# Two head projections of a gated attention layer as the row halves of one product

## The chip, the cores and the metric

The kernel runs on one core of a Trainium2 chip. The metric is the device time of one execution in microseconds (us); where several executions are given, their median counts. A core has five engines that run their own instruction streams and meet on semaphores: TensorE (PE, matrix products into PSUM; its weight loads are listed as PEld), VectorE (DVE), ScalarE (ACT), GpSimd (POOL) and SyncE (SP), which here only starts transfers.

## What is computed

A network of two layers on an input of 4 sequences of 1024 tokens of 256 values. The change lies in the second layer's attention (`L1_attn`), of which this is the part that matters:

```python
x = _ln(x, ln1_w, ln1_b)                  # 4 x 1024 x 256
qk = _silu(x @ Wqk.T + bqk)               # 64 values a token
v = _silu(x @ Wv.T + bv)                  # 512 values a token
heads = qk[..., None, :] * gamma + beta   # four heads of 64
quad_q, lin_q, quad_k, lin_k = map(_rope, ...)
quad_att = einsum('bgid,bgjd->bgij', qq, qkk) / G + bias   # groups of 64 tokens
attn = relu(quad_att) ** 2
lin_kv = einsum('bgnd,bgne->bde', lk, vg) / n
gate = _silu(x @ Wg.T + bg)
out = (gate * (quad_out + lin_out)) @ Wo.T + bo            # then layer norm
```

`_rope(h)` is `h * cos + swapped(h) * sin` with the two halves of the 64 values exchanged in `swapped` (and a sign in `sin`). So every head needs the activated projection straight and swapped. Beside the attention the second layer has eight experts, of which each token takes two, with low-rank additions; the first layer has a causal attention and a wide feed-forward part. The sum of all is the output.

## The kernel before

All matrix products of the parts named here are fp32 split in a high and a low part (fp32r), so that one product of a 128-row block is three matmuls; with an input of 256 values (two chunks `c`) a product of 512 columns is six matmuls at L1554 (helper `times`).

The work runs in stages that follow one another on each engine: the first layer (`layer0`), the second layer's attention for sequences 2 and 3 (`attention(..., half=0)`, about 450 to 590 us of the span), the experts over 71 tiles of 128 gathered rows (`moe`, about 590 to 940 us), and the attention for sequences 0 and 1 (`half=1`, about 940 us to the end). The order inside a stage is written by hand: for each engine a table lists units such as `VV:3` or `QK:1` (`ATTENTION_UNITS`, and `TURN` where the first layer's end and the first attention half are interleaved). Within a half the two sequences make four blocks `n` of 512 tokens. The units that matter:

- `UT`: transposition of the normed rows, PE then ACT (high part) and DVE (low part, L1783) into `uT`.
- `VV:n` (16 a half): the value product of 128 tokens, DVE adds the bias (L1809), ACT applies Silu (L1721).
- `GA:n` (16 a half): the gate product of a block, ACT applies Silu into `gT` (L1729).
- `QK:n` and `QR:n` (4 each a half): the head projection, straight (`QK`, columns 0 to 127 of `wqk1`) and swapped (`QR`, columns 128 to 255). Each is 128 rows, since the 64 values stand there twice, for two heads. ACT applies Silu into `q` or `r` (L1718) and so gives the PSUM bank back.
- `QC:n`, `RS:n` (DVE, L1788): `q` times the cosine table, `r` times the sine table, in place.
- `HA:n`, `HB:n` (DVE, L1801 and L1803): `headA` and `headB` as `q*gamma + offset`, then `+ r*gamma_swapped`. `headA` holds the two query heads on partitions 0 to 63 and 64 to 127, `headB` the two key heads.
- `KT:n` (PE, L1583): `headB` is transposed; `AT:n` (L1616): the attention inside groups; `LK:n` (L1624): the sum over keys and values of a whole sequence, which waits for all eight `VV` and both `KT` of it; `OO:n` (L1634, L1637) the output rows, `YY:n` (L1648) the output projection.
- `YS`, `YF` (DVE, L1837 to L1858): the layer norm behind `YY`. Each odd `YS` has a step on POOL too, a power at L1496.
- `XB` (DVE, L1814): a bias onto the rows that the result is added to.
- `BP`, `WH`, `WL`, `FB` (first half only): the norm's weight and bias are folded into the weights.
- `GX`, `GZ` (POOL, L1486, second half only): 64 gathering transfers, each adding the expert results of 128 rows onto the rows in SBUF. POOL issues them in the order of its table, with the `YS` steps in between.

The products rotate over six PSUM banks in the order of PE's table (`g_use`): a product waits until the one six places ahead of it has been taken from its bank by ACT or DVE.

## Time and profile before

| | |
|---|---|
| median of 3 runs | 1089.68 us (1088.37 to 1092.4) |
| time of the profiled execution | 1089.73 us |
| its span | 1088.1 us |
| TensorE busy | 1050.9 us (97%) |
| VectorE busy | 797.1 us (73%) |
| ScalarE busy | 387.2 us (36%) |
| GpSimd busy | 432.8 us (40%) |
| granted TensorE clock, mean | 0.991 |

The span is measured inside the profiled execution; its time holds another 1.6 us around it. The busy share of an engine is the union of its instructions. Matmuls overlap in the pipeline, so the duration of one (some 390 ns at L1554) is longer than the step from one to the next. A line of a timeline gives the start, the time covered, the engine, source line, operation, the tile written and the tiles read, the count, and in brackets how long the engine had been idle before and what it had waited for.

### The profile page before, as it was taken

The numbers are of one execution on the slowest core, as the hardware profiler recorded it, in microseconds if no ns is written. First come the engines' busy times: TensorE is split into PE (matmuls) and PEld (weight loads), VectorE is DVE, ScalarE is ACT, GpSimd is POOL, SyncE is SP. The second block draws the span as 40 slices with busy tenths as digits, with TensorE's granted clock in tenths as the row PEclk, the third lists the DMA queues.
The fourth block names the chain that finished last, engine by engine and source line by source line (L and its number), as shares of the span: only waits on it lengthen the run. The fifth ranks groups of instructions, "written<-read, shape, count | busy, mean of one in ns | idle before, by whom it ended". The sixth has DMA issues, their size and how long they took to land.

```text
span 1088.1 us, 20660 instructions
## 1 busy us (share of the span) xinstructions
PE 1050.9 (97%) x6206; PEld 903.1 (83%) x6206; DVE 797.1 (73%) x1842; ACT 387.2 (36%) x786; POOL 432.8 (40%) x408
## 2 busy tenths in 40 slices
PE   5999999999999999999999999999999999999995
PEld 4898889887989798967877888888888888878874
DVE  5667987788788877787857877777777777754745
ACT  2644454445353535443311232323222232432300
POOL 2834666565756575163202110101001000188876
PEclk9999999999999999999999999999999999999998
DMA  8333444543445337321144565515345241355556
GB/s 253 102 117 127 139 148 141 181 161 127 157 166 175 113 134 234 120 72 41 52 142 141 199 214 170 199 50 199 103 146 192 93 161 52 113 99 89 86 79 145
DMA packets 87254, 147.83 MB, mean 136 GB/s; under 512 B 8432, under 2 KB 64624, under 8 KB 87024
## 3 DMA queue, kind: packets, MB, share of 16 engines
q1 hardware_dynamic: 66416, 98.24, 27.9%
q0 software_dynamic: 20736, 48.28, 16.1%
q8 instruction: 57, 0.93, 0.4%
q14 instruction: 45, 0.37, 0.1%
HBM read 89.04 MB, written 57.45 MB: 135 GB/s over the span
## 4 chain that ended last, share of the span: by engine, by line
PE 70%; DVE 13%; issue 7%; POOL 6%; DMA 2%; ACT 0%; DVEq 0%; POOLq 0%; ACTq 0%
PE wide L2073 18%; PE wide L592 12%; PE bank L592 11%; PE bank L2073 9%; PE bank L2098 3%; POOL first_half L1486 3%; PE wide L1554 3%; DVE hT L1022 2%; PE wide L1648 2%; PE bank L1554 2%; POOL x_second L1486 2%; PE bank L2066 1%; PE wide L1624 1%; DMA x1b<-slot_results_scratch,result_rows 1%; POOL x1b L1486 1%
## 5 line engine op out<-in xcount | busy, mean ns | idle before, releaser
L2073 PE MATMUL wide<-expert_ring,xsT 128*128 x852 | 228.5, 403 | 1.5 <-DVE xsT L2162 0.8
L2073 PEld LDWEIGHTS wide<-expert_ring,xsT 128*128 128x128 f32 x852 | 150.1, 188 | 29.3 <-issue 3.0
L2131 ACT ACTIVATE gsT<-bank 128x512 fp32r<-128x512 f32 x71 | 42.5, 599 | 243.6 <-PE bank L2098 243.6
L1946 POOL DMA_DIRECT2D expert_ring<-experts_scratch x24 | 17.1, 712 | 253.2 <-DVE slots_h L2180 186.1
L2073 PEld LDWEIGHTS bank<-expert_ring,gsT 128*128 128x128 f32 x852 | 112.1, 189 | 6.6 <-issue 0.3
L2073 PE MATMUL bank<-expert_ring,gsT 128*128 x852 | 114.0, 282 | 0.1
L2174 DVE TENSOR_TENSOR slots_h<-wide,expert_bias 128x512 f32<-128x512 f32 x71 | 49.1, 691 | 73.3 <-PE wide L2073 73.1
L563 POOL TENSOR_TENSOR folded_matrix<-fold,folded_matrix 128x512 fp32r<-128x512 f32 x48 | 64.1, 1341 | 60.6 <-ACT folded_matrix L778 60.4
L576 POOL DMA_INDIRECT slot_rows_scratch<-u,slot x64 | 66.8, 1044 | 50.1 <-issue 20.6
L592 PE MATMUL bank<-w,hT 128*128 128x264 f32 x480 | 61.5, 285 | 0.5 <-DVE hT L1022 0.5
L592 PEld LDWEIGHTS bank<-w,hT 128*128 128x128 f32 x480 | 59.5, 188 | 0.8 <-issue 0.7
L592 PE MATMUL wide<-xnT,pT 128*128 128x512 f32 (+2 forms) x288 | 59.1, 352 | 0.0
L1486 POOL DMA_INDIRECT x1b<-slot_results_scratch,result_rows x16 | 27.3, 1707 | 74.2 <-DVE x1b L1814 68.9
L2162 DVE TENSOR_TENSOR gsT<-bank,gsT 128x512 fp32r<-128x512 f32 x71 | 49.0, 690 | 9.5 <-ACT gsT L2131 1.5
L2183 DVE SCALAR_TENSOR_TENSOR slots_g<-slots_h,xs_ring,slots_h 128x512 f32<-128x512 f32 x71 | 53.4, 752 | 2.5
L1486 POOL DMA_INDIRECT first_half<-slot_results_scratch,result_rows x32 | 51.3, 1604 | 9.7 <-issue 9.3
L1022 DVE TENSOR_TENSOR hT<-hid,hT 128x512 fp32r<-128x512 f32 x64 | 53.4, 840 | 2.1 <-ACT hid L834 1.9
L2180 DVE TENSOR_TENSOR slots_h<-wide,expert_bias 128x512 f32<-128x512 f32 x71 | 49.1, 691 | 7.0 <-PE wide L2073 1.7
L592 PEld LDWEIGHTS wide<-xnT,pT 128*128 128x128 f32 x288 | 48.2, 190 | 6.3 <-issue 0.2
L592 PE MATMUL bank<-xnT,w 128*128 128x512 f32 x192 | 51.1, 409 | 0.0
L592 PE MATMUL wide<-xnT,w 128*128 128x512 f32 x192 | 50.8, 406 | 0.0
L1496 POOL TENSOR_TENSOR rsy<-vey,half 128x2 f32<-128x2 f32 x16 | 16.8, 1049 | 78.1 <-DVE vey L1846 78.1
(313 smaller groups left out, 2398.8 us busy)
## 6 DMA issues: line engine op xcount, KB each, us to landing
experts_scratch<-folded_matrix SPq DMA_DIRECT2D x24, 1024.0 KB, 5.2
expert_ring<-experts_scratch POOLq DMA_DIRECT2D x24, 1024.0 KB, 5.6
raw<-in_expert_weights SPq DMA_DIRECT2D x24, 512.0 KB, 6.2
xs_ring<-slot_rows_scratch SPq DMA_DIRECT2D x71, 128.5 KB, 2.4
slot_results_scratch<-ys_ring SPq DMA_DIRECT2D x71, 128.0 KB, 2.4
lora<-in_expert_lora SPq DMA_DIRECT2D x24, 288.0 KB, 3.1
u<-in_L_attn_x SPq DMA_DIRECT2D x4, 1024.0 KB, 5.3
expert_bias<-in_expert_bias POOLq DMA_DIRECT2D x8, 512.0 KB, 7.0
```

Of the source, the lines that this page charges most:

```text
L563: tt(fold_part(n, 1), fold[:, n % 2, :], fold_part(n, 0), ALU.subtract).then_inc(matrix_ready, 1)
L576: nc.gpsimd.indirect_dma_start(out=scr["xs"], in_=xb[:, b % 2, t, 0:ROW], in_offset=None, bounds_check=SLOTS - 1, out_offset=bass.Indirect ...
L592: ins = mm(o, stationary(i), moving(j), start=(first and q == 0), stop=(last and q == 2))
L1022: tt(hT[:, 1, n % IC, :], hid[:, n % 2, :], hT[:, 0, n % IC, :], ALU.subtract).then_inc(hid_low, 1)
L1486: nc.gpsimd.indirect_dma_start(out=target, out_offset=None, in_=scr["ys"], in_offset=index(k, tile_at), bounds_check=SLOTS_T * P - 1, comp ...
L1554: ins = mm(o, stationary(i), moving(j), start=(first and k == 0), stop=(last and k == 2))
L2073: ins = mm(o, parts[i], moving, start=(first and q == 0), stop=(last and q == 2))
L2131: return nc.scalar.activation(o, i, ACT.Copy)
L2162: tt(flat[1], bank, flat[0], ALU.subtract).then_inc(taken, 1)
L2174: tt(h1[:, j % 2, :], H[j % 2][0], bias(e, 0, HID), ALU.add).then_inc(h1_ready, 1)
L2180: tt(h3[:, i, :], H[i][1], bias(e, HID, HID), ALU.add).then_inc(h_taken, 1)
L2183: stt(out=g[:, i, :], in0=h1[:, i, :], scalar=xs[:, j % ROUND, DIM:ROW], in1=h3[:, i, :], op0=ALU.mult, op1=ALU.mult).then_inc(g_ready, 1)
```

## The change

`WEIGHTS1` gives `wqk1` 128 columns instead of 256: the 64 straight columns and then the 64 swapped ones (`heads_first`). The units `QR` are gone from all tables. One product `QK:n` of six matmuls gives the straight projection on partitions 0 to 63 and the swapped one on 64 to 127. ACT takes that bank three times: whole into `q`, the upper half into the lower half of `r`, the lower half into the upper half of `r`; the bank is given back behind the third. So `q` holds straight and swapped values, `r` swapped and straight ones, and the tables (`turn`), the scale and offset columns (`head_columns`) and the biases are laid out to fit: cosine and sine are mixed over the partitions in the same way. `headA` and `headB` hold what they held. In the tables `QK:n` stands mostly where `QR:n` or `QK:n` stood first; the DVE table is unchanged, and so are POOL's and SP's.

```diff
-WEIGHTS1 = (("wqk1", 4 * QK), ("wv1", H1), ("wg1", H1))
+WEIGHTS1 = (("wqk1", 2 * QK), ("wv1", H1), ("wg1", H1))
...
-            elif kind in ("QK", "QR"):
+            elif kind == "QK":
                 rows_split(n)
                 weight_split(0)
                 o, done = g_bank(un)
-                at = slice(0, P) if kind == "QK" else slice(P, 2 * P)
                 for c in range(DC):
-                    last = times(o, lambda i: wqk1[:, i, c, at], lambda i: uT[:, i, c, n % 2 * 512:(n % 2 + 1) * 512],
+                    last = times(o, lambda i: wqk1[:, i, c, :], lambda i: uT[:, i, c, n % 2 * 512:(n % 2 + 1) * 512],
                                  c == 0, c == DC - 1)
...
-                    for k in range(2):
-                        for c in range(DC):
-                            last = mm(S[:, 512 + EC + k:513 + EC + k], raw["wqk1"][:, c, k * P:(k + 1) * P],
-                                      cols[:, 2 + c:3 + c], start=(c == 0), stop=(c == DC - 1))
+                    for c in range(DC):
+                        last = mm(S[:, 512 + EC:513 + EC], raw["wqk1"][:, c, :], cols[:, 2 + c:3 + c],
+                                  start=(c == 0), stop=(c == DC - 1))
...
-            elif kind in ("QK", "QR"):
-                to, bias = (q, cols[:, 8:9]) if kind == "QK" else (r, cols[:, 9:10])
+            elif kind == "QK":
                 if n >= 2:
                     act.wait_ge(headB_ready, H0 + n - 1)
-                nc.scalar.activation(to[:, n % 2, :], g_full(act, un), ACT.Silu, bias=bias).then_inc(g_free(un)[0], 1)
+                both, lower, upper = g_full(act, un), slice(0, QK), slice(QK, P)
+                nc.scalar.activation(q[:, n % 2, :], both, ACT.Silu, bias=cols[:, 8:9])
+                nc.scalar.activation(r[lower, n % 2, :], both[upper], ACT.Silu, bias=cols[upper, 8:9])
+                nc.scalar.activation(r[upper, n % 2, :], both[lower], ACT.Silu, bias=cols[lower, 8:9]).then_inc(g_free(un)[0], 1)
...
             elif kind in ("QC", "RS"):
                 to = q if kind == "QC" else r
-                dve.wait_ge(*g_free(("QK" if kind == "QC" else "QR", n)))
+                dve.wait_ge(*g_free(("QK", n)))
```

PE's rows at the start of the first attention half, before (`wv`, `wg` and `wqk` with a number are the split weights; the first row is `QR:0`, the last `QR:1`; behind it come `VV:6`, `VV:7` and `KT:0`):

```order
L1554 MATMUL wide<-uT,wqk_92 128x512 x6
L1554 MATMUL wide<-wv_93,uT 128x512 x6
L1576 MATMUL bank<-ident,u 128x128 x4
L1554 MATMUL wide<-wv_93,uT 128x512 x6
L1554 MATMUL bank<-uT,wqk_92 128x512 x6
L1554 MATMUL bank<-uT,wg_94 128x512 x6
L1554 MATMUL wide<-uT,wqk_92 128x512 x6
L1554 MATMUL wide<-uT,wg_94 128x512 x6
L1554 MATMUL wide<-wv_93,uT 128x512 x12
L1554 MATMUL bank<-uT,wg_94 128x512 x6
L1554 MATMUL bank<-wv_93,uT 128x512 x6
L1554 MATMUL wide<-uT,wqk_92 128x512 x6
```

The same place now, from `QK:0` to `KT:0`:

```order
L1553 MATMUL wide<-uT,wqk_92 128x512 x6
L1553 MATMUL wide<-wv_93,uT 128x512 x6
L1575 MATMUL bank<-ident,u 128x128 x4
L1553 MATMUL wide<-wv_93,uT 128x512 x6
L1553 MATMUL bank<-uT,wg_94 128x512 x6
L1553 MATMUL bank<-uT,wqk_92 128x512 x6
L1553 MATMUL wide<-uT,wg_94 128x512 x6
L1553 MATMUL wide<-wv_93,uT 128x512 x12
L1553 MATMUL wide<-uT,wg_94 128x512 x6
L1553 MATMUL bank<-wv_93,uT 128x512 x12
L1553 MATMUL wide<-wv_93,uT 128x512 x6
L1582 MATMUL bank<-ident,headB 128x128 x4
```

The first two pairs of projections are two products now: `QK:0` stands in the place of `QR:0`, `GA:0` stands ahead of `QK:1` and a place earlier, and from `VV:0` to `KT:0` there are thirteen products where fifteen were.

ACT's rows at the same place, before (the first two `v_52` rows are `VV:0` and `VV:1`):

```order
L1721 ACTIVATE v_52<-v_52 128x512 x2
L1718 ACTIVATE r<-wide,cols_79 128x512
L1729 ACTIVATE gT<-bank,cols_79 128x512
L1718 ACTIVATE q<-bank,cols_79 128x512
L1721 ACTIVATE v_52<-v_52 128x512
L1718 ACTIVATE q<-wide,cols_79 128x512
L778 ACTIVATE folded_matrix<-fold 128x512
```

and now:

```order
L1720 ACTIVATE v_52<-v_52 128x512 x2
L1715 ACTIVATE q<-wide,cols_79 128x512
L1716 ACTIVATE r<-wide,cols_79 64x512
L1717 ACTIVATE r<-wide,cols_79 64x512
L1728 ACTIVATE gT<-bank,cols_79 128x512
L1720 ACTIVATE v_52<-v_52 128x512
L1715 ACTIVATE q<-bank,cols_79 128x512
L1716 ACTIVATE r<-bank,cols_79 64x512
L1717 ACTIVATE r<-bank,cols_79 64x512
L778 ACTIVATE folded_matrix<-fold 128x512
```

Two passes of a pair on two banks have become three passes on one bank, one behind the other.

PE's rows at the start of the second attention half, before, from `VV:0`, `VV:1` to `KT:0`:

```order
L1554 MATMUL wide<-wv_93,uT 128x512 x12
L1554 MATMUL wide<-uT,wqk_92 128x512 x6
L1576 MATMUL bank<-ident,u 128x128 x8
L1554 MATMUL wide<-uT,wqk_92 128x512 x6
L1554 MATMUL bank<-wv_93,uT 128x512 x12
L1554 MATMUL wide<-uT,wqk_92 128x512 x6
L1554 MATMUL wide<-wv_93,uT 128x512 x6
L1554 MATMUL wide<-uT,wqk_92 128x512 x6
L1554 MATMUL wide<-uT,wg_94 128x512 x6
L1554 MATMUL bank<-wv_93,uT 128x512 x6
L1583 MATMUL bank<-ident,headB 128x128 x4
```

and now:

```order
L1553 MATMUL wide<-wv_93,uT 128x512 x12
L1553 MATMUL bank<-uT,wqk_92 128x512 x6
L1575 MATMUL bank<-ident,u 128x128 x8
L1553 MATMUL bank<-wv_93,uT 128x512 x6
L1553 MATMUL wide<-wv_93,uT 128x512 x6
L1553 MATMUL wide<-uT,wqk_92 128x512 x6
L1553 MATMUL wide<-wv_93,uT 128x512 x6
L1553 MATMUL wide<-uT,wg_94 128x512 x6
L1553 MATMUL bank<-wv_93,uT 128x512 x6
L1582 MATMUL bank<-ident,headB 128x128 x4
```

Two of the ten products ahead of `KT:0` are gone.

## Rows read from the trace of the kernel before

**Rows 1.** The page: busy time of each engine, its share of the span, instructions.

```profile
PE 1050.9 (97%) x6206; PEld 903.1 (83%) x6206; DVE 797.1 (73%) x1842; ACT 387.2 (36%) x786; POOL 432.8 (40%) x408
```

**Rows 2.** Timeline of PE, first half, first sequence of it.

```profile
449.00 0.95 PE L1659 MATMUL wide<-cols,wqk_raw 128*128 128x1 f32 x8
...
466.65 2.88 PE L1554 MATMUL wide<-wv,uT 128*128 128x512 f32 x12
...
477.03 0.66 PE L1583 MATMUL bank<-ident,headB 128*128 128x128 f32 x4 [0.70 <-DVE headB L1803]
```

**Rows 3.** Timeline of DVE, same stretch.

```profile
454.85 0.69 DVE L1783 TENSOR_TENSOR uT<-bank,uT 128x512 fp32r<-128x512 f32 x1 [0.37 <-ACT uT L1676]
...
466.94 0.68 DVE L1788 TENSOR_TENSOR q<-q,turn 128x512 f32<-128x512 f32 x1
...
474.39 2.59 DVE L1803 SCALAR_TENSOR_TENSOR headB<-r,cols,headB 128x512 f32<-128x512 f32 x1
```

**Rows 4.** Timelines of ACT and of POOL (the last row), same stretch.

```profile
464.38 0.67 ACT L1718 ACTIVATE r<-wide,cols 128x512 f32<-128x512 f32 x1
464.95 0.68 ACT L1729 ACTIVATE gT<-bank,cols 128x512 f32<-128x512 f32 x1
...
489.11 0.59 ACT L1676 ACTIVATE lkv<-wide 64x512 f32<-64x512 f32 x1 [7.63 <-PE wide L1624]
...
475.12 1.30 POOL L563 TENSOR_TENSOR folded_matrix<-fold,folded_matrix 128x512 fp32r<-128x512 f32 x1
```

**Rows 5.** Timelines of DVE and PE (the last row), second sequence, first half.

```profile
529.53 0.69 DVE L1809 TENSOR_TENSOR v<-wide,bv 128x512 f32<-128x512 f32 x1 [0.77 <-PE wide L1554]
...
538.07 0.69 DVE L1809 TENSOR_TENSOR v<-wide,bv 128x512 f32<-128x512 f32 x1 [0.29 <-PE wide L1554]
...
544.11 0.75 DVE L1803 SCALAR_TENSOR_TENSOR headB<-r,cols,headB 128x512 f32<-128x512 f32 x1
...
545.81 0.60 PE L1583 MATMUL bank<-ident,headB 128*128 128x128 f32 x4
```

**Rows 6.** Timelines of DVE and PE (the last row), start of the second half.

```profile
955.65 0.75 DVE L1803 SCALAR_TENSOR_TENSOR headB<-r,cols,headB 128x512 f32<-128x512 f32 x1
...
958.75 0.60 PE L1583 MATMUL bank<-ident,headB 128*128 128x128 f32 x4
```

**Rows 7.** Timeline of POOL, second half: the gathers and the power steps.

```profile
948.23 1.69 POOL L1486 DMA_INDIRECT x1b<-slot_results_scratch,result_rows  x1 [68.94 <-DVE x1b L1814]
...
1054.41 1.56 POOL L1486 DMA_INDIRECT x_second<-slot_results_scratch,result_rows  x1 [0.31 <-issue]
1058.43 0.88 POOL L1496 TENSOR_TENSOR rsy<-vey,half 128x2 f32<-128x2 f32 x1 [2.47 <-DVE vey L1846]
1059.51 1.88 POOL L1486 DMA_INDIRECT first_half<-slot_results_scratch,result_rows  x1 [0.20 <-issue]
...
1069.11 1.55 POOL L1486 DMA_INDIRECT x_second<-slot_results_scratch,result_rows  x1 [0.30 <-issue]
1071.28 0.72 POOL L1496 TENSOR_TENSOR rsy<-vey,half 128x2 f32<-128x2 f32 x1 [0.61 <-DVE vey L1846]
1072.64 1.59 POOL L1486 DMA_INDIRECT first_half<-slot_results_scratch,result_rows  x1 [0.64 <-issue]
1074.53 1.57 POOL L1486 DMA_INDIRECT first_half<-slot_results_scratch,result_rows  x1 [0.30 <-issue]
...
1077.04 1.80 POOL L1486 DMA_INDIRECT first_half<-slot_results_scratch,result_rows  x1 [0.18 <-DMA first_half<-slot_results_scratch,result_rows]
```

**Rows 8.** PE's timeline, first layer; last row a window: us, busy times, clock, DMA.

```profile
270.22 0.44 PE L719 MATMUL bank<-ident,res 128*128 128x128 f32 x2 [1.56 <-DVE res L970]
...
375.61 0.69 PE L719 MATMUL bank<-ident,res 128*128 128x128 f32 x2 [1.54 <-DVE res L970]
376.07 4.28 PE L592 MATMUL wide<-xnT,w 128*128 128x512 f32 x12
...
377.00:378.00 1.00, 1.00 (x4) 0.71 (x3) 0.85 (x4) 0.62 (x2) 0.00 (x0) 0.50 0.02 4
```

## What is expected of the change

> **What bounds the kernel now.** I read the page first, then the waits of TensorE, the chain by stretches, and the timelines of all engines where the change lies. The page says that PE is busy for 97% of the span [rows 1], so a product less looks like its full price. The timelines say where that fails. From 482 us to 590 us and through the experts to 944 us PE runs with hardly a gap: what comes earlier there is handed on in full. At two places another engine ends last. In the first sequence of the first half DVE has no gap to speak of from 457 us on, and PE already waits 0.70 us at `KT:0` for `headB` [rows 2]. And in the second half the chain that ended last is no longer PE's but POOL's: 64 gathers of some 1.56 us with 0.30 us between them, from 948.23 us to the end [rows 7]. PE is done there at about 1076 us, POOL at 1081 us, and the last stores follow POOL. So the first half is read on PE and DVE, the second on POOL.
>
> **The change, part by part.** A product of six matmuls: from the start of `VV:3` at 466.65 to the end of the work ahead of `KT:0` (477.03 less the wait of 0.70) lie seven products, 9.68 us [rows 2], so 1.38 us each. Eight `QR` go: 8 x 1.38 = 11.0 us of PE work. `BP:0` halves, from 0.95 us for its 8 records [rows 2]: 0.4 us more. On the path:
>
> (a) `BP:0`, 0.4 us. DVE waits 0.37 us for the transposed rows behind it (PE, then ACT) [rows 3], so DVE's chain moves with PE: 0.4 us, and some 0.1 us more of short waits for `VV` there, 0.5 us.
>
> (b) `QR:0` and `QR:1`, 2.76 us on PE. Both lie ahead of `KT:0`, which needs `headB`. DVE's work up to there is what it was, and its second step of `HB:0` ends at 474.39 + 2.59 = 476.98 us [rows 3]. PE waits instead. `VV:3` starts at 465.8 us (the third pass, below), six products follow from it on, 6 x 1.38 = 8.3 us, and PE is at `KT:0` at 474.1 us, where `headB` comes at 476.98 - 0.5 = 476.5 us: a wait of 2.4 us in the place of 0.70. Gain: 0. Of the 2.59 us, 1.84 are a meeting with a step of POOL at 475.12 to 476.42 us [rows 4]; the usual duration of this line is 0.75 us [rows 5]. Moves of 0.1 us decide whether they meet again; if not, `RS:1` or `HB:1` meet it and `KT:1` waits, so at most some 0.5 us of it come through. The trace shows only that the two overlap. The Trainium skill (GPSIMD Engine Reference, "1. Specifications") states that GpSimd shares its SBUF interfaces with VectorE where a VectorE instruction has two inputs in SBUF, as this one has; by it the meeting costs the same wherever it falls, and the sum would stay; the row agrees with it, in one case.
>
> (c) The three passes. A pass starts 0.57 us behind the one before (464.38, 464.95) and takes 0.67 us [rows 4]. A pass on 64 partitions, PSUM to SBUF, took 0.59 us [rows 4], so half the partitions save nothing and I take 0.57 us a step. No row shows one that reads one half of the partitions and writes the other. Its bounds are 0.57 us, the plain step, and twice that; I take the plain one, which is nearest in every other respect. ACT then gives the bank of `QK:0` back at 464.0 + 3 x 0.57 + 0.1 = 465.8 us. `QC:0` on DVE comes at 466.94, 466.5 after the shift [rows 3]: not late, by 0.7 us. Twice the price for two passes would use that up, with 0.4 us lost. `VV:3`, now six places behind `QK:0`, waits for that bank until 465.8 us, and `GA:0`, moved up, waits about 1.3 us for its split weights. Both waits lie inside (b). ACT is at 36% [rows 1]; eight passes more, 4.6 us, delay nothing else.
>
> (d) `QR:2` and `QR:3`, 2.76 us. PE would reach `KT:3` at 545.81 - 2.76 = 543.05 us; `headB` is there at 544.11 + 0.75 = 544.86 us [rows 5]. DVE comes earlier by its waits for PE: 0.77 and 0.29 us [rows 5] make 543.80 us, and the waits too short to be listed make at best 543.3 us. PE then waits 0.25 to 0.75 us: 2.0 to 2.5 us remain, and I take 2.4.
>
> First half: 0.5 + 2.4 = 2.9 us (2.5 to 3.5). The experts hand it on, and so does the start of POOL's gathers, which follow `XB:0` and so `VV:0` of the second half.
>
> (e) Second half. At its start PE reaches `KT:0` at 958.75 us, `headB` is ready at 955.65 + 0.75 = 956.40 us [rows 6]. Without two products PE is there at 955.99; the third pass may hold `QC:0` up by up to 0.4 us: a wait of up to 0.8 us. The other two come through whole (there DVE follows PE). So PE and what follows it run 5.5 - 0.8 = 4.7 us earlier. But POOL ends last. It waits for PE's side twice. Step from gather to gather over a power step: 5.10 us (1054.41 to 1059.51) and 3.53 us (1069.11 to 1072.64), against 2.51 us where nothing was waited for (1074.53 to 1077.04) [rows 7]. Without the waits: 2.59 + 1.02 = 3.6 us. To lift both, DVE's variance must come 3.6 us sooner, and 4.7 us are there. The remaining 1.1 us buy nothing.
>
> Sum: 2.9 + 3.6 = 6.5 us. The profiled execution took 1089.73 us with a span of 1088.1 us, and the median is 1089.68, so 1089.7 - 6.5 = **1083.2 us**, 0.6% less.
>
> **The rivals.** *The clock falls at the new wait.* In the first layer a wait of 1.54 us was followed by 0.50 of the clock (1.2 instead of 2.4 GHz), and twelve matmuls took 4.28 us [rows 8] where twelve of the same shape take 2.88 [rows 2]: 1.4 us, and with the few behind them until the clock is back 1.7 us. A like wait of 1.56 us at 270.22 was not followed by it [rows 8], a third one at 163.40 us was. The wait of 2.4 us at `KT:0` is longer than each, and it lies on PE's path: 6.5 - 1.7 = 4.8 us of gain remain, 1084.9 us. Against it: if `HB:0` escapes POOL's step, the wait falls apart into two short ones. [...]
>
> *POOL's chain does not shorten.* If something else holds the power steps (the landing of the gathers, of which the wait at 1077.04 speaks [rows 7], or a late `YF` on DVE), the second half gives under 1 us, and 2.9 to 3.5 us remain in all: 1086.5 us.
>
> *The full price.* If DVE had slack at `KT:0` after all, the first half would give 5.9 us and the second still only 3.6: 1080.2 us.
>
> *Slower: the shifted passes are dear.* Each costs x us more than a plain one; `QC:n` gets late by 2x where a block is waited for, at `QC:0` of both halves. With the slack of 0.7 us in the first half and none in the second, the first half loses 2x - 0.7, and the second, behind its reserve of 1.1 us, 2x - 1.1. The kernel is slower by over 0.5% where 4x - 1.8 is over 6.5 + 5.4, so from x = 3.4 us on: with x = 4 us, 1089.7 - 6.5 + 14.2 = 1097.4 us. Against it speaks the pass of 0.59 us on half the partitions.
>
> *The change does less than it says*: the products are gone from PE's list by the order, so this one has no chance worth a number.
>
> **How the numbers follow.** Forecast (1082.2 to 1084.2) 0.45; the clock, 1084.9, 0.30; POOL's chain, 1086.5, 0.13; full price, 0.07; slower, 0.05. The range holds the first three with the spread of the runs' medians by a microsecond: 1081.2 to 1087.6. A measurement of this kernel can tell about 0.5%, 5.4 us, from no change. Below 1084.3 lie most of the forecast, the full price and a little of the clock's case: 0.50. Over 0.5% slower 0.05, the rest 0.45.
>
> **What would show it.** Right: in the first half a wait of PE at `KT:0` of 2 to 2.5 us for `headB`, at `KT:3` one under 1 us; ACT's three passes 0.57 us apart and all of 0.6 to 0.7 us; the experts start 2.5 to 3.5 us earlier; POOL's power steps in the second half without a wait for DVE, and a span from the first gather to the last store some 3.6 us shorter. PE's 11 us less work show as idle time. Wrong: a granted clock of 0.50 right behind `KT:0`; a shifted pass well over 0.7 us; waits at 1058 us and 1071 us still there; or PE waiting at a bank.

## The result, and the profile after

The changed kernel takes 1087.19 us (median of 20 runs, 1082.88 to 1089.46), the kernel before beside it 1090.88 us (20 runs, 1088.37 to 1093.51). The ratio is 0.996, with a 95% interval of 0.9948 to 0.9971: a gain of 3.7 us, 0.4%. 6.5 us were forecast, and 1083.2 us. Of the 4.0 us between the two times, 1.2 us are the median of before, which was 1089.68 us in the three runs that the forecast started from; 2.8 us are the effect.

The profiled execution of the changed kernel took 1088.44 us, with a span of 1086.8 us and a mean granted clock of 0.981 (before: 1089.73, 1088.1 and 0.991). The page, as [rows 1]:

```profile
PE 1044.9 (96%) x6154; PEld 896.6 (83%) x6154; DVE 798.4 (73%) x1842; ACT 393.8 (36%) x794; POOL 432.9 (40%) x408
```

TensorE is busy 6.0 us less, not 11.4. Where the other 5 us are is the story of this case. PE's timeline in the first sequence of the first half (as [rows 2]):

```profile
464.10 1.62 PE L1553 MATMUL bank<-uT,wg 128*128 128x512 f32 x6 [1.33 <-DVE wg L1757]
...
468.77 3.00 PE L1553 MATMUL wide<-wv,uT 128*128 128x512 f32 x12 [0.31 <-ACT r L1717]
...
479.23 0.82 PE L1582 MATMUL bank<-ident,headB 128*128 128x128 f32 x4 [2.02 <-DVE headB L1802]
479.99 2.08 PE L1614 MATMUL wide<-headA,headB 64*128 64x128 f32 x8
481.99 2.93 PE L1553 MATMUL wide<-uT,wg 128*128 128x512 f32 x6
484.71 1.06 PE L1582 MATMUL bank<-ident,headB 128*128 128x128 f32 x4
```

The waits are the forecast ones: `GA:0` 1.33 us for its weights, `VV:3` for the third pass, `KT:0` 2.02 us for `headB`. But behind `KT:0` the durations double: six matmuls of `GA:3` take 2.93 us, where `GA:0` takes 1.62. The windows of that stretch (us, their length, busy time with count of PE, PEld, DVE, ACT and POOL, granted clock, DMA share, GB/s) say why:

```profile
477.00:479.00 2.00, 0.21 (x1) 0.00 (x0) 2.00 (x1) 0.00 (x0) 1.82 (x3) 1.00 0.19 66
479.00:481.00 2.00, 1.77 (x8) 1.45 (x9) 2.00 (x4) 0.91 (x2) 1.05 (x1) 0.65 0.18 66
481.00:483.00 2.00, 2.00 (x7) 1.59 (x7) 1.71 (x8) 0.64 (x2) 0.00 (x0) 0.50 0.00 0
483.00:485.00 2.00, 2.00 (x7) 1.50 (x6) 1.26 (x9) 0.20 (x1) 1.30 (x2) 0.50 0.03 12
485.00:487.00 2.00, 2.00 (x9) 1.71 (x8) 1.47 (x6) 0.60 (x1) 1.16 (x2) 0.65 0.15 53
```

PE stood still from 477.21 to 479.23 us, and right behind it the granted clock is 0.50, that is 1.2 instead of 2.4 GHz, until some 486 us. Slow matmuls count as busy time: that is where the 5 us are, 3.1 us between `KT:0` and `LK:0` and 1.7 us in the first layer, ahead of `UT:1`. There the mean granted clock was 0.97 over the first 448 us in this execution and 0.99 in that of before, and `UT:1` came 2.5 us later (451.03 against 448.56 us).

DVE's timeline of `HB:0` (as [rows 3]), and POOL's row at that time (as [rows 4]):

```profile
475.74 0.74 DVE L1800 SCALAR_TENSOR_TENSOR headB<-q,cols,offset 128x512 f32<-128x512 f32 x1
476.63 2.55 DVE L1802 SCALAR_TENSOR_TENSOR headB<-r,cols,headB 128x512 f32<-128x512 f32 x1
```

```profile
477.34 1.28 POOL L563 TENSOR_TENSOR folded_matrix<-fold,folded_matrix 128x512 fp32r<-128x512 f32 x1
```

The second step met POOL's step again and took 2.55 us instead of 0.75. The meeting repeats because POOL's chain hangs on DVE's: the seven scatters (indirect stores) ahead of the fold wait for DVE's `u` (L1012). The first of them starts at 467.47 us and the fold 9.87 us behind it; in the kernel before it is 465.29 us and 9.83 us. So POOL's chain moves with DVE's.

ACT's timeline, the three passes of `QK:0` and the one behind them (as [rows 4]):

```profile
466.56 0.67 ACT L1715 ACTIVATE q<-wide,cols 128x512 f32<-128x512 f32 x1
467.24 0.69 ACT L1716 ACTIVATE r<-wide,cols 64x512 f32<-64x512 f32 x1
467.94 0.68 ACT L1717 ACTIVATE r<-wide,cols 64x512 f32<-64x512 f32 x1
468.65 0.69 ACT L1728 ACTIVATE gT<-bank,cols 128x512 f32<-128x512 f32 x1
```

Each is as long as a plain pass, but the starts lie 0.68 to 0.71 us apart, not 0.57.

`KT:3` in the second sequence on PE, and the DVE step that it needs (as [rows 5]):

```profile
548.57 0.66 PE L1582 MATMUL bank<-ident,headB 128*128 128x128 f32 x4
```

```profile
547.76 0.75 DVE L1802 SCALAR_TENSOR_TENSOR headB<-r,cols,headB 128x512 f32<-128x512 f32 x1
```

`headB` ends at 548.51 us, 0.06 us ahead of its use: DVE has become the equal of PE there, and no wait is listed. `KT:0` of the second half (as [rows 6]) waits as forecast:

```profile
959.70 0.66 PE L1582 MATMUL bank<-ident,headB 128*128 128x128 f32 x4 [0.87 <-DVE headB L1802]
```

POOL's timeline in the second half, at the two power steps that waited before (as [rows 7]):

```profile
1056.49 1.55 POOL L1485 DMA_INDIRECT x_second<-slot_results_scratch,result_rows  x1 [0.30 <-issue]
1057.55 1.28 POOL L1495 TENSOR_TENSOR rsy<-vey,half 128x2 f32<-128x2 f32 x1
1059.01 1.59 POOL L1485 DMA_INDIRECT first_half<-slot_results_scratch,result_rows  x1 [0.18 <-issue]
...
1068.60 1.55 POOL L1485 DMA_INDIRECT x_second<-slot_results_scratch,result_rows  x1 [0.30 <-issue]
1069.70 1.21 POOL L1495 TENSOR_TENSOR rsy<-vey,half 128x2 f32<-128x2 f32 x1
1071.10 1.79 POOL L1485 DMA_INDIRECT first_half<-slot_results_scratch,result_rows  x1 [0.19 <-issue]
```

Gather to gather over a power step is 2.52 and 2.50 us; it was 5.10 and 3.53. Both waits are gone.

To compare executions whose first layers differ, I cut each span at five instructions: PE's transposition of `UT:1` (the last mark ahead of which the change moves nothing), `KT:0`, `LK:0`, the experts' first transposition of `slots_g`, POOL's first gather of the second half. The table gives the microseconds between their starts, and to the end of the span. A dagger marks kernels that ran on another chip, on which the kernel before took 1112.79 us and 1111.97 us in the two sets of runs; there `UT:1` starts at 468 to 473 us instead of 447 to 453, and the stages behind it look as on the first chip (`plain` beside the changed kernel). The kernel before has no trace on that chip. Each row is one execution, and the ends of the spans are read to 0.1 us.

| kernel | UT:1 to KT:0 | to LK:0 | to experts | to first gather | to end | UT:1 to end | wait at KT:0 |
|---|---|---|---|---|---|---|---|
| before | 28.47 | 5.01 | 112.54 | 353.65 | 139.9 | 639.5 | 0.70 |
| after | 28.20 | 8.14 | 110.02 | 353.49 | 135.9 | 635.8 | 2.02 |
| `fill` | 28.24 | 5.01 | 110.03 | 353.36 | 135.5 | 632.2 | 0.70 |
| `dup_first` | 29.54 | 6.58 | 112.66 | 353.40 | 135.7 | 637.9 | 2.03 |
| `dup_second` | 28.18 | 6.55 | 110.00 | 353.48 | 140.1 | 638.3 | 2.03 |
| `order` | 26.01 | 4.86 | 114.02 | 353.47 | 136.6 | 634.9 | none |
| `dup_both` † | 28.89 | 5.02 | 113.44 | 353.60 | 140.0 | 641.0 | 1.38 |
| `plain` † | 28.06 | 8.14 | 110.02 | 353.52 | 135.0 | 634.7 | 2.03 |
| `es10` † | 26.39 | 5.02 | 111.01 | 353.48 | 135.5 | 631.4 | 0.23 |
| `before_es10` † | 27.65 | 4.93 | 113.26 | 353.60 | 139.7 | 639.1 | none |
| `order2` † | 24.96 | 3.67 | 116.79 | 353.44 | 135.8 | 634.7 | none |
| `order3` † | 24.99 | 3.67 | 115.23 | 353.48 | 135.4 | 632.8 | none |

From before to after: 0.3 us gained up to `KT:0`, 3.1 lost up to `LK:0`, 2.5 gained up to the experts, 0.2 in them, 4.0 behind the first gather. The sum is 3.8 us (the last column says 3.7, for rounding), and the medians say 3.7.

### The profile page after: what moved, and what is told of

It reads as the page before. It is cut to its first block, busy times and chain, and to the rows that moved or that the text cites. A ratio compares the mean times of both kernels' runs of the same rounds, so it can differ in the third digit from the quotient of the medians.

```text
span 1086.8 us, 20552 instructions
## 1 busy us (share of the span) xinstructions
PE 1044.9 (96%) x6154; PEld 896.6 (83%) x6154; DVE 798.4 (73%) x1842; ACT 393.8 (36%) x794; POOL 432.9 (40%) x408
## 4 chain that ended last, share of the span: by engine, by line
PE 68%; DVE 14%; POOL 6%; issue 6%; DMA 4%; ACT 1%; DVEq 0%; POOLq 0%; SPq 0%; ACTq 0%
PE wide L2072 19%; PE wide L592 11%; PE bank L592 11%; PE bank L2072 9%; PE wide L1553 3%; PE bank L2097 3%; POOL first_half L1485 3%; DVE hT L1022 2%; PE wide L1646 2%; DMA x_second<-slot_results_scratch,result_rows 2%; POOL x1b L1485 2%; PE bank L2065 1%; PE bank L1622 1%; POOL x_second L1485 1%; PE bank L1553 1%
## 5 line engine op out<-in xcount | busy, mean ns | idle before, releaser
L2072 PEld LDWEIGHTS wide<-expert_ring,gsT 128*128 128x128 f32 x852 | 112.1, 189 | 6.6 <-issue 0.3
L2072 PE MATMUL wide<-expert_ring,xsT 128*128 x432 | 115.9, 404 | 0.9 <-DVE xsT L2161 0.8
L2072 PE MATMUL wide<-expert_ring,gsT 128*128 x852 | 114.0, 282 | 0.1
L2072 PE MATMUL bank<-expert_ring,xsT 128*128 x420 | 112.8, 403 | 0.5 <-issue 0.5
L2072 PEld LDWEIGHTS wide<-expert_ring,xsT 128*128 128x128 f32 x432 | 76.1, 188 | 15.1 <-issue 1.8
L2072 PEld LDWEIGHTS bank<-expert_ring,xsT 128*128 128x128 f32 x420 | 74.0, 188 | 14.1 <-issue 1.1
L2173 DVE TENSOR_TENSOR slots_h<-wide,expert_bias 128x512 f32<-128x512 f32 x36 | 24.9, 692 | 39.5 <-PE wide L2072 39.5
```

What stands on the lines that cost most here:

```text
L2072: ins = mm(o, parts[i], moving, start=(first and q == 0), stop=(last and q == 2))
L2173: tt(h1[:, j % 2, :], H[j % 2][0], bias(e, 0, HID), ALU.add).then_inc(h1_ready, 1)
```

## The experiments

The theory after the result: the products are worth their price but for those ahead of `KT:0`, which turn into a wait for DVE; that wait is 2 us mostly because of the meeting with POOL, and the low clock behind it costs 3.1 us. The rival theories: the loss between `KT:0` and `LK:0` has nothing to do with the wait; the passes cost something; the second half's gain is not due to the products.

**`fill`: one product more, in the place of the wait.**

```diff
             elif kind == "VV":
...
-                for c in range(DC):
-                    last = times(o, lambda i: uT[:, i, c, tile(n)], lambda i: wv1[:, i, c, :], c == 0, c == DC - 1)
+                for turn_of in range(2 if half == 0 and n == 7 else 1):
+                    for c in range(DC):
+                        last = times(o, lambda i: uT[:, i, c, tile(n)], lambda i: wv1[:, i, c, :], c == 0, c == DC - 1)
```

> The changed kernel, but the value product VV:7 of the first half, the last one ahead of KT:0, is issued twice: 1.38 us of PE work put into the wait of 2.0 us. Theory (the long wait brings the clock to 0.50 for 6.8 us, at a cost of 3.1 us): the wait shrinks to some 0.6 us, the clock stays at 1.00 behind it, and the stretch from the transposition at some 451 us to POOL's first gather falls from 499.9 to some 496.8 us; in all 2 to 3 us faster than the changed kernel where that had the low clock. Rival (the clock falls anyway, or the time is lost to DVE): no shorter stretch, since PE does more work and not less.

Measured: 1084.53 us against 1090.84 for the kernel before, ratio 0.994 (0.9925 to 0.9956). PE's timeline, and one window of it:

```profile
477.08 2.88 PE L1553 MATMUL wide<-wv,uT 128*128 128x512 f32 x12
480.66 0.66 PE L1582 MATMUL bank<-ident,headB 128*128 128x128 f32 x4 [0.70 <-DVE headB L1803]
481.24 1.16 PE L1615 MATMUL wide<-headA,headB 64*128 64x128 f32 x8
482.33 1.68 PE L1553 MATMUL wide<-uT,wg 128*128 128x512 f32 x6
```

```profile
481.00:483.00 2.00, 2.00 (x14) 1.61 (x13) 1.85 (x4) 1.12 (x2) 0.47 (x1) 1.00 0.19 66
```

`KT:0` comes as long after `UT:1` as in the changed kernel (28.24 and 28.20 us), so the product costs nothing; the wait is 0.70 instead of 2.02 us, the clock stays at 1.00, and `KT:0` to `LK:0` takes 5.01 instead of 8.14 us. The kernel with more work on its busiest engine is faster, by 3.6 us from `UT:1` to the end. That shows where the missing gain is: the low clock behind the wait, 3.1 us in the traces. The medians give a smaller difference, 0.994 against 0.996 of the kernel before (2.2 us), and the two intervals overlap; each kernel has one trace, so how often the clock falls there, and for how long, in its other executions isn't known.

**`dup_first` and `dup_second`: the QK product twice in one half.** The products go back to one half, the tables and the three passes stay (the second diff has `half == 1`).

```diff
-                for c in range(DC):
-                    last = times(o, lambda i: wqk1[:, i, c, :], lambda i: uT[:, i, c, n % 2 * 512:(n % 2 + 1) * 512],
-                                 c == 0, c == DC - 1)
+                for turn_of in range(2 if half == 0 else 1):
+                    for c in range(DC):
+                        last = times(o, lambda i: wqk1[:, i, c, :], lambda i: uT[:, i, c, n % 2 * 512:(n % 2 + 1) * 512],
+                                     c == 0, c == DC - 1)
```

> The changed kernel, but each projection product of the first attention half is issued twice into the same bank (six matmuls more for each of the four blocks), so PE has there the work that it had before; ACT's three passes stay, and the second half stays as changed. Theory (the first half gives nothing because PE only waits instead and then runs at half clock, the second gives what POOL's chain gives): the wait at KT:0 shrinks from 2.0 to some 0.3 to 0.7 us, no clock of 0.50 behind it, the stretch from the first transposition that follows the first layer's products (351 us after the start, some 451 us) to POOL's first gather is as long as before (500 us) or 0.4 us shorter, the stretch from the first gather to the end is as in the changed kernel, 135.9 us against 139.9 before: 3.5 to 4 us faster than before in all, so no slower than the changed kernel. Rival (the passes on ACT cost the first half its gain): the stretch to the first gather is longer than before by 2 us or more.

> The changed kernel, but each projection product of the second attention half is issued twice, so PE has its old work there; the first half stays as changed. Theory (in the second half PE's earlier arrival lifts POOL's two waits for the power steps): the waits of 2.5 and 0.6 us come back, and the stretch from POOL's first gather to the end is 139 to 140 us, as before, against 135.9 in the changed kernel; in all 3.5 to 4 us slower than the changed kernel, as slow as before within 1 us. Rival (the second half got shorter for another reason, such as fewer meetings of DVE and POOL): the stretch stays at 136 to 137 us.

Measured: `dup_first` 1088.67 us, ratio 0.9974 (0.9959 to 0.9989); `dup_second` 1090.43 us, ratio 0.9998 (0.9985 to 1.0011), against 1090.84.

`dup_second` says that the second half's gain is the products': with them back, first gather to end is 140.1 us as before (139.9), and POOL's waits at the two power steps are there again (1.28 us at 1057.80, 0.62 at 1070.65). A third one, 2.20 us at 1000.38, is in neither of the two kernels; in all POOL waits 4.1 us for power steps, 3.1 us before. `dup_first` leaves that gain whole (135.7 us) and takes back the 2.6 us of the second sequence (112.66 us from `LK:0` to the experts). But it missed at `KT:0`: the wait stayed at 2.03 us and the clock fell behind it, for 3.4 us instead of 6.8. DVE's timeline says why:

```profile
461.20 0.69 DVE L1809 TENSOR_TENSOR v<-wide,bv 128x512 f32<-128x512 f32 x1 [0.42 <-PE wide L1553]
...
468.88 0.69 DVE L1788 TENSOR_TENSOR q<-q,turn 128x512 f32<-128x512 f32 x1 [0.31 <-ACT r L1718]
```

The second product lies between `VV:0` and `VV:1`, ahead of `UT:3`, where only one of before's two stood. So DVE waits 0.42 us for `VV:1`, then 0.31 us for the third pass and 0.46 us for `VV:3`, and its own chain ends later: `KT:0` is 29.54 us behind `UT:1`, over a microsecond later than in either of the two kernels. A product is cover only if what the waiting engine needs does not lie behind it.

**`dup_both`: TensorE's work of before, the three passes of after.**

> Every QK product is issued twice, in both halves: TensorE's work is that of the kernel before in all but BP:0, DVE's the same, and only ScalarE's three passes are new. If the passes cost nothing, the time is within 1 us of the kernel before, 1090 to 1091.5, and POOL's waits of 1 and 2.5 us are back. If the three passes hold something up (QC:0 in the second half by 0.4 us a pass over 0.57), it is over 1092.

Measured: 1112.98 us against 1112.79, ratio 1.0005 (0.9983 to 1.0028). The passes have no price that the runs can tell from nothing. The trace has `UT:1` to the end 1.5 us longer than before, of which 0.4 lie ahead of `KT:0` (the waits of `dup_first`) and 0.9 between `LK:0` and the experts; so "nothing" holds within about 1.5 us, and where the products are gone the third pass holds PE at `VV:3` for 0.31 us, inside the longer wait (1.23 us in `order`, below, where ACT takes that bank later). The wait at `KT:0` was 1.38 us, and the clock stayed up.

**`es10`: POOL's step out of the way.** One unit in POOL's table, the fold of the first expert columns, is moved behind two scatters and `ZR:0`.

```diff
-        SC:6@3 ES:10@3 SC:7@3 SC:8@3 ZR:0 SC:9@3 ...
+        SC:6@3 SC:7@3 SC:8@3 ZR:0 ES:10@3 SC:9@3 ...
```

> One unit of POOL, the fold of the first expert columns of 128x512 (1.28 us, which overlaps DVE's second step of HB:0), stands behind three others, some microseconds later; all else as in the changed kernel. If the overlap is what stretches that step from 0.75 to 2.55 us, the step takes 0.75 us here, headB is ready 1.7 us earlier, the wait at KT:0 is 0.3 to 0.5 us in the place of 2.0, TensorE's clock stays at 1.00 behind it, and the time is 1084 to 1085.5. If the step is slow for another reason it stays at 2.5 us and the time at 1087. A third case: the fold meets a step of HB:1 or RS:1 instead, and KT:1 waits 1 to 2 us.

Measured: 1104.31 us against 1112.79, ratio 0.993 (0.9902 to 0.9959). The expected 1084 to 1085.5 us were for the first chip; by the stages it is 631.4 us from `UT:1`, 4.4 less than the changed kernel and 8.1 less than before, and the ratio says 7.8 us. Against the changed kernel the ratios say 3.3 us (0.993 and 0.996), and their intervals overlap. DVE's timeline, POOL's and PE's:

```profile
496.85 0.75 DVE L1802 SCALAR_TENSOR_TENSOR headB<-r,cols,headB 128x512 f32<-128x512 f32 x1
...
505.04 1.76 DVE L1824 SCALAR_TENSOR_TENSOR att<-attw 128x512 f32<-128x512 f32 x1 [0.15 <-DVE attw L1820]
```

```profile
504.96 1.28 POOL L563 TENSOR_TENSOR folded_matrix<-fold,folded_matrix 128x512 fp32r<-128x512 f32 x1
```

```profile
497.65 0.66 PE L1582 MATMUL bank<-ident,headB 128*128 128x128 f32 x4 [0.23 <-DVE headB L1802]
```

The step of `HB:0` takes 0.75 us, the wait is 0.23, and the clock stays. POOL's step now stretches the one of DVE that it falls on, `att` (1.76 us instead of 0.69), which nobody waits for behind the 7 us of `LK:0`. So the overlap is what stretches a step, and where it falls decides the price. Of the 4.4 us, 1.8 come ahead of `KT:0`, 3.1 are the clock, 0.4 come at the end, and 1.0 is given back between `LK:0` and the experts, where `YY:0` now waits 0.76 us.

The stretched steps have one thing in common: each ended 0.55 to 0.56 us behind POOL's step, in all ten traces in which POOL's step met `headB` or `att` in the first sequence. So the price is the time from DVE's usual end to POOL's end, and some half a microsecond. Not every meeting costs DVE that. The changed kernel has another one in the second sequence, DVE's rows and POOL's:

```profile
541.17 0.68 DVE L1787 TENSOR_TENSOR r<-r,turn 128x512 f32<-128x512 f32 x1
541.77 0.69 DVE L1808 TENSOR_TENSOR v<-wide,bv 128x512 f32<-128x512 f32 x1
542.37 1.18 DVE L1787 TENSOR_TENSOR q<-q,turn 128x512 f32<-128x512 f32 x1
```

```profile
541.20 1.80 POOL L563 TENSOR_TENSOR folded_matrix<-fold,folded_matrix 128x512 fp32r<-128x512 f32 x1 [9.00 <-ACT folded_matrix L778]
```

Here POOL starts 0.03 us behind `r`; `r` keeps its 0.68 us, and POOL's own step takes 1.80 us instead of 1.28. `v`, with one input in PSUM (`wide`), runs wholly beside it in its usual 0.69 us. `q`, with both inputs in SBUF, takes 1.18 us instead of 0.68 and ends 0.55 us behind POOL's step. So one of the two engines waits, now DVE and now POOL. What decides isn't shown: in the first sequence POOL's step had begun 0.71 us behind `headB` and still it was `headB` that was stretched, and there a scatter of POOL (476.31 to 477.33 us) had been running when `headB` began. By the Trainium skill (GPSIMD Engine Reference, "1. Specifications") GpSimd shares its SBUF interfaces with VectorE where a DVE instruction has two inputs in SBUF; these rows agree with it.

**`before_es10`: the same move in the kernel before.**

> The kernel before with the fold of POOL moved behind the same three units. There TensorE waits 0.70 us at KT:0 for headB, of whose last step 1.84 us are the overlap. If the chain of DVE is what eats the two products, moving the fold gives this kernel only the 0.70 us, 0.1% (ratio 0.999 to 1.000), and the changed kernel with the fold moved stands 0.6 to 0.7% below it. If moving the fold is a gain of its own that has nothing to do with the products (the transfers of POOL behind it, or KT:1), this kernel gains 2 us or more too (0.998 or less).

Measured: 1107.91 us against 1111.97, ratio 0.9979 (0.9958 to 1.0001). The interval holds both theories' numbers, and its middle, 2.3 us, is the rival's. The trace speaks for the theory. From `UT:1` to the end it takes 639.1 us, 0.3 to 0.4 less than before: `KT:0` comes 0.8 us sooner, and 0.7 us are given back between `LK:0` and the experts, 0.52 of them in a wait at `YY:0`. `dup_both` has such a wait too (0.53 us) on the same chip, where the kernel before has no trace, so a part of what is given back may be the chip's.

By the traces, both of one chip, the products are worth 7.7 us beside the moved fold (639.1 to 631.4), against 3.7 without the move: the meeting had eaten half of what the change brings. That size rests on single traces; the ratios (0.993 and 0.9979, so 0.5%, against 0.4% for the change alone) are too coarse to show it. Even so only 1.3 us of the 2.76 ahead of `KT:0` came (27.65 to 26.39 us). At `KT:0` PE waits just 0.23 us in `es10`, but ahead of it 1.33 us at `GA:0` for DVE's split weights and 0.32 us at `VV:3` for the third pass.

**`order`: DVE's work for `headB` first.** `HB:0` moves ahead in DVE's table, `OF:0` and `HA:0` behind `VV:7`, `WL:2` ahead of `VV:0`; on PE `AT:0`, which needs `headA`, goes behind `LK:0`.

```diff
-        ... VV:7 KT:0 AT:0 GA:3 KT:1 GA:4 LK:0 GA:5 OO:0 ...
+        ... VV:7 KT:0 GA:3 KT:1 GA:4 LK:0 AT:0 GA:5 OO:0 ...
...
-        ... UT:2 CH:1@3 VV:0 VV:1 WL:2 UT:3 TG:0@3
-        N1:2@3 N1:3@3 VV:2 OF:0 QC:0 RS:0 VV:3 OF:1 HA:0 VV:4 VV:5 QC:1 HB:0 RS:1 VV:6 HB:1 VV:7 TH:0@3 ...
+        ... UT:2 CH:1@3 WL:2 VV:0 VV:1 UT:3 TG:0@3
+        N1:2@3 N1:3@3 VV:2 QC:0 RS:0 VV:3 OF:1 HB:0 VV:4 VV:5 QC:1 RS:1 VV:6 HB:1 VV:7 OF:0 HA:0 TH:0@3 ...
...
                 hold(dve, v_held, turned, 2 * (H0 + n) + 2)
+                if half == 0 and n == 0:
+                    hold(dve, v_held, offset_step, 2 - p)
```

> The changed kernel with its first half in another order at the start: on DVE the low part of the gate weights ahead of VV:0, HB:0 directly behind the offset of headB, and OF:0 and HA:0 behind VV:7; on PE AT:0 behind LK:0. So what KT:0, KT:1 and LK:0 need comes up to 2.8 us earlier on DVE. Theory (DVE's chain up to headB and the values, and the clock behind the wait for it, take the first sequence's gain): no wait at KT:0 over 0.7 us, no clock of 0.50 there, LK:0 starts 4 to 6 us earlier against the transposition at some 451 us than in the changed kernel (36.3 us there), and the whole is 4 to 6 us faster than the changed kernel, 1081 to 1083 us. Rival (POOL's step that DVE meets, or ACT, ends last): LK:0 moves by under 2 us.

Measured: 1084.12 us against 1090.84, ratio 0.9945 (0.9927 to 0.9964). PE's timeline (the first row is `KT:1`; `KT:0` doesn't wait):

```profile
476.39 0.66 PE L1582 MATMUL bank<-ident,headB 128*128 128x128 f32 x4 [0.91 <-DVE headB L1804]
...
488.45 1.10 PE L1632 MATMUL wide<-headA,lkv 128*128 128x512 f32 x2 [0.32 <-DVE att L1826]
...
494.01 1.13 PE L1632 MATMUL wide<-headA,lkv 128*128 128x512 f32 x2 [1.82 <-ACT gT L1728]
```

`LK:0` starts 30.87 us behind `UT:1`, 5.5 sooner than in the changed kernel, but 4.0 us of that are given back up to the experts: `AT:0` now lies behind `LK:0` (1.1 us), and the products behind it wait 0.32 us for `att` and 1.82 us for `gT`. No wait reached 2 us, and the clock stayed up. The expected gain of `LK:0` came, that of the whole did not: by the stages 0.9 us over the changed kernel, where 4 to 6 were expected, and the ratios, 0.9945 and 0.996, have intervals that overlap.

**`order2` and `order3`: the new waits chased.** `order2` is `order` with DVE's table `AT:0 HA:1 F1:0@3 OO:0 OO:1 OO:2 TB:2 OO:3 TB:3` where `AT:0 TB:2 OO:0 F1:0@3 HA:1 OO:1 OO:2 TB:3 OO:3` stood, and with `QK:0` ahead of `VV:0` in ACT's table. `order3` adds the move of `es10` and puts POOL's `F1:0@3` ahead of its last three scatters.

> The kernel with the new order, and two changes more. DVE's units behind AT:0 stand as HA:1, F1:0, OO:0, OO:1, OO:2 and only then TB:2, so that the gates' buffers come free earlier; ACT takes QK:0's bank ahead of the Silu of VV:0 and VV:1. If the two waits behind LK:0 (0.32 and 1.82 us) and that at VV:3 (1.23 us) were what was left of the first sequence's cost, PE waits under 0.5 us at each, from UT:1 to the first gather of the second half lie 495.5 to 496.5 us instead of 498.4, and the median is 1082 to 1083. If DVE's work there only moves the wait (to UT:4, which needs F1:0, or to OO:4), it stays at 1084.

> The second version of the new order with the fold of POOL moved behind ZR:0, and POOL's power step of F1:0 ahead of its last three scatters of rows and of ZR:1, so that u and with it UT:4 come earlier. If the waits at UT:4 (1.73 us) and at YY:0 (1.07 us), and the low clock behind them, were all that ate the order's gain, TensorE has no wait of over 0.5 us from VV:0 to KT:3, from UT:1 to the first gather lie 493 to 494.5 us, and the ratio is 0.990 to 0.992, below the 0.993 of the changed kernel with the moved fold. If POOL's scatters, now later, hold up the experts' first gather, or the last steps of DVE take over, it is 0.993 to 0.995.

Measured (the times expected were again for the first chip, so the stages count): `order2` 1107.06 us against 1112.79, ratio 0.995 (0.9927 to 0.9973); `order3` 1103.23 us against 1111.97, ratio 0.9918 (0.9886 to 0.995). PE's timeline of `order2`:

```profile
523.19 0.65 PE L1575 MATMUL bank<-ident,u 128*128 128x128 f32 x4 [1.73 <-ACT u L1673]
524.91 3.64 PE L1646 MATMUL wide<-wo,oT 128*128 128x256 f32 x8 [1.07 <-issue]
```

Both missed by their stages: from `UT:1` to the first gather they take 498.9 and 497.4 us. The ratio of `order3`, 0.9918, lies in its expected range all the same. In `order2` the wait moved to `UT:4`, as the second case had it, but through POOL and not DVE: `LK:0` is 7.7 us sooner than in the changed kernel, and the experts start only 0.9 us sooner, since `UT:4` waits for `u`, which waits for a power step of POOL that stands behind all its scatters, and `YY:0` at half the clock takes 3.64 us. In `order3` the waits are 1.43 us (`u`) and 1.40 (`att`), the clock stays up, and the stage from `UT:1` to the experts is 143.9 us; `es10`, with one unit moved, has 142.4. By the ratios, 0.9918 and 0.993, the two can't be told apart. Both are faster than the kernel before and, by the stages, than the changed one.

**`plain`: where the passes' step comes from.** In the first half the two passes on 64 partitions stay on their half; in the second half `r` is one pass on 128. `r` isn't swapped then, so the output is another one.

```diff
-                nc.scalar.activation(r[lower, n % 2, :], both[upper], ACT.Silu, bias=cols[upper, 8:9])
-                nc.scalar.activation(r[upper, n % 2, :], both[lower], ACT.Silu, bias=cols[lower, 8:9]).then_inc(g_free(un)[0], 1)
+                if half == 0:
+                    nc.scalar.activation(r[lower, n % 2, :], both[lower], ACT.Silu, bias=cols[lower, 8:9])
+                    nc.scalar.activation(r[upper, n % 2, :], both[upper], ACT.Silu, bias=cols[upper, 8:9]).then_inc(g_free(un)[0], 1)
+                else:
+                    nc.scalar.activation(r[:, n % 2, :], both, ACT.Silu, bias=cols[:, 8:9]).then_inc(g_free(un)[0], 1)
```

> The output is another one: r isn't swapped. In the first half the two passes on 64 partitions read and write the same half of the partitions; in the second half r is one pass on all 128. If the shift to the other partitions makes the step of 0.69 us, it is 0.57 us in both halves. If passes on 64 partitions do, it is 0.69 in the first half and 0.57 us in the second. If passes that read one bank behind each other do, it is 0.69 us in both.

Measured, ACT's timeline in both halves:

```profile
483.50 0.67 ACT L1715 ACTIVATE q<-wide,cols 128x512 f32<-128x512 f32 x1
484.07 0.67 ACT L1717 ACTIVATE r<-wide,cols 64x512 f32<-64x512 f32 x1
484.76 0.68 ACT L1718 ACTIVATE r<-wide,cols 64x512 f32<-64x512 f32 x1
485.47 0.69 ACT L1731 ACTIVATE gT<-bank,cols 128x512 f32<-128x512 f32 x1
...
969.37 0.69 ACT L1715 ACTIVATE q<-bank,cols 128x512 f32<-128x512 f32 x1
969.94 0.70 ACT L1720 ACTIVATE r<-bank,cols 128x512 f32<-128x512 f32 x1
970.51 0.65 ACT L1723 ACTIVATE v<-v 128x512 f32<-128x512 f32 x1
```

The second expectation is the nearest, but none holds as it was put. One bank read twice is no cause (0.57 us in the second half), nor are 64 partitions as such (0.57 us from `q` to the lower half). The step is 0.69 to 0.71 us to and from the pass on the upper 64 partitions, although it is not shifted. In the changed kernel the first pass behind `q` reads the upper half and the second writes it, and all three steps are 0.68 to 0.71 us. So both kernels fit one reading: a step is 0.11 to 0.14 us longer where one of the two passes reads or writes partitions 64 to 127 alone. They fit another one as well: that it is longer where the first partition changes from one pass to the next, from 0 to 64 or back. No run tells the two apart, nor the reading from the writing side.

## Why the prediction was wrong in its size and right in most of its steps

1083.2 us were forecast and 1087.19 measured, within the range of 1081.2 to 1087.6. A gain of 0.4% is inside the 0.5% called no change, to which 0.45 were given; 0.5 had gone to faster. That the time lies in the range is in part luck: its upper end stood there for the case that POOL's chain does not shorten, which did not come, and 1.2 us of the distance are the median of before.

(a) Up to `KT:0`, 0.5 us forecast, 0.27 gained. `BP:0` did get 0.4 us shorter, but the transposition of `UT:2` came only 0.29 us sooner behind `UT:1` (4.70 instead of 4.99 us), since `BP:1` and `BP:2` between them took 0.16 us longer, and DVE's chain moved by no more than that.

(b) The products ahead of `KT:0`, forecast at nothing. The waits were as forecast: 2.02 us (2.4 said; with steps of 0.70 us between the passes `VV:3` started 0.5 us later than forecast), `GA:0` 1.33 (1.3), `VV:3` waiting for the third pass. The meeting with POOL's step came again, but not for the reason given: "moves of 0.1 us decide" is wrong, since POOL's chain starts at a step of DVE and moves with it; and a meeting doesn't cost the same wherever it falls (1.8 us at `headB`, 1.1 us at `att`, 0.5 us of POOL's time at `r`). **This is the step that failed**, not by what it named but by where it stopped: "PE waits instead. Gain: 0" takes the wait as free of consequences in the sum. It wasn't nothing but a loss of 3.1 us, since the clock fell behind it. That was the first rival, with a chance of 0.30 and a price of 1.7 us. The chance was too low. The price came from a row in the first layer where the clock was at 0.50 for 3.4 us (375.33 to 378.74 us), and for such a stretch it is right: in `dup_first` and `dup_second`, with 3.4 us at 0.50, `KT:0` to `LK:0` took 6.58 and 6.55 us instead of 5.01. In the changed kernel and in `plain` the clock was at 0.50 for 6.8 us (479.58 to 486.41 us in the changed kernel), and the stretch took 8.14 us. So the cost is a little under half of the time at half the clock, and the term that was mis-sized is that time. Why it is 6.8 us in two traces and 3.4 in two others behind the same wait stays open. The 3.1 us are 2.8 us of missing effect and a little that other terms gave back.

The chance can now be put beside rows. Waits of PE in the attention and what the clock did behind them:

| kernel | wait, us | granted clock behind it |
|---|---|---|
| after, `dup_first`, `dup_second`, `plain` | 2.02, 2.03, 2.03, 2.03 at `KT:0` | 0.50 |
| `order2` | 1.73 ahead of 523.19 us and 1.07 ahead of 524.91 | 0.50 |
| `order` | 1.82 at `OO:2` | 1.00 |
| `order3` | 1.43 ahead of 520.78 us and 1.40 ahead of 524.59 | 1.00 |
| `dup_both` | 1.38 at `KT:0` | 1.00 |
| after, `es10`, `fill`, `dup_second`, `plain` | 1.33 to 1.35 at `GA:0` | 1.00 |
| before, `fill` | 0.70 at `KT:0` | 1.00 |

In the attention this reads: the fall behind all four waits of 2 us, behind none of 1.43 us or less by itself, and either in between. The first layer [rows 8] says that it is a chance and not a limit. At its row L719 PE waits 1.52 to 1.57 us three times in each of the twelve traces; the clock fell in the wait or within 1.7 us behind it in 25 of these 36 cases, and at the same place in one trace and not in another. On the second chip the first layer has longer waits too, 1.78 to 4.69 us: the fall came at 23 of 24, but not at the one of 2.12 us ahead of 181.82 us in `order2`. The forecast wait of 2.4 us lay above every wait that it was compared with, of which two in three had the fall, and a chance over one half would have followed from that. The Trainium skill (TensorE: Matmul & The Clock Gate, "Why this matters for your kernels") warns of idle gaps between bursts of matmuls and gives a length, which no wait of the attention reaches. The first layer's waits beyond it, on the second chip, agree; but waits of 2.0 us were followed by the fall four times out of four here, so the measurement decides, and the advice is too generous for this kernel.

(c) The passes cost nothing that the times can tell, as forecast (0.31 us at `VV:3` lie inside the longer wait); the step was 0.70 us, not 0.57, within its bounds of 0.57 and twice that. The pass of 0.59 us on 64 partitions [rows 4] was the wrong neighbour: it was on the lower ones and stood alone.

(d) `QR:2` and `QR:3`: 2.4 us forecast (2.0 to 2.5), 2.5 gained. The wait of 0.25 to 0.75 us at `KT:3` was too short to be listed; DVE followed PE closer than its listed waits said.

(e) The second half: 3.6 us forecast, 4.0 gained, by the mechanism named. `KT:0` waits 0.87 us (up to 0.8 said), POOL's two waits are gone, and `dup_second` brings them back. By the rows of the gathers the two steps give 3.6 us, and some 0.6 us come early in the chain, where a gather waits 0.44 us (959.04 us) and not 1.13 us for one to land (957.39 us before); that part wasn't forecast, and 0.2 us are lost again behind it. PE's side gained more than POOL could use, which `es10` shows too: it changes nothing behind the first gather (135.5 us).

Of the other rivals, POOL's chain did shorten, the full price did not come, and the shifted passes were not dear: a step was some 0.12 us more than a plain one, and the 3.4 us from which that case decides were far off.

## What to carry to other kernels

A product less on the busiest engine, ahead of a wait that is already there, is not simply worth nothing: it makes the wait longer, and behind the longer wait the clock can fall, so that it costs. Look for what stretches the late engine's chain (here one step of GpSimd beside one of VectorE, 1.8 us of a late `headB`), move that, and only then take the products out; if nothing can be moved, a product kept as filler ahead of the wait can be faster than none. And where a wait disappears by a new order, look at what it let other engines do: `order2` gained 7.7 us at one place and kept 0.9.

## What the runs showed of the hardware that I had not expected

- The low clock behind a wait of 2.0 us can cost more than the wait: 3.1 us from `KT:0` to `LK:0` in two traces with 6.8 us at 0.50, 1.5 to 1.6 us in two others with 3.4 us at 0.50 behind the same wait.
- A fp32 step of DVE on 128x512 that runs beside POOL's step of 128x512 (1.28 us) becomes 1.9 to 2.6 us long instead of 0.75 where both of its tensor inputs are in SBUF: 2.55 us where POOL started 0.71 us behind it, 1.98 in `order` where it started 0.12 us behind. It ends 0.55 to 0.56 us behind POOL's step. `v<-wide,bv`, with one input in PSUM, kept its 0.69 us beside such a step, and at `r<-r,turn` it was POOL's step that got longer, 1.80 us.
- ACT's passes follow one another in 0.57 us, and in 0.68 to 0.71 us around one that reads or writes only the upper 64 partitions.
